# Two 16-head attention stages on one core: row maxima subtracted by another engine in layer 0, output sums joined differently in layer 1

## The reference

```python
# layer 0
scores = jnp.einsum('bhsd,bhtd->bhst', q, k) * scale
attn = jax.nn.softmax(scores, axis=-1)
out = jnp.einsum('bhst,bhtd->bhsd', attn, v)      # then times WO
# layer 1: rotary q and k, and a bias by distance
dist = jnp.abs(pos[None, :] - pos[:, None])
kb = -p * jnp.log1p(a * dist)
attn = jax.nn.softmax(scores + kb[None], axis=-1)
out = jnp.einsum('bhqk,bhkd->bhqd', attn, v)      # then times out_w.T
```

## Time and profile before

| what | value |
|---|---|
| median of three runs | 3134.81 us |
| the profiled execution's own time | 3134.13 us |
| its span, first to last instruction | 3132.3 us |
| mean granted TensorE clock | 0.962 |
| busy: PE / DVE / ACT / POOL | 2869.8 / 2307.5 / 1428.2 / 2439.6 us |
| attention in layer 0, first to last exponential | 239.3 to 1449.3 us |
| attention in layer 1, first to last exponential | 1815.0 to 3107.4 us |

### The profile page before, as it was taken

One profiled execution on the slowest core, in us unless ns is written; L12 is line 12 of the kernel. 1 busy time (PEld: TensorE's weight loads), 2 busy tenths in 40 slices (PEclk: granted clock), 3 DMA queues, 4 the chain that ended last, 5 costly groups with the idle time before them and its releaser, 6 DMA issues. The chain is left out here.

```text
span 3132.3 us, 46995 instructions
## 1 busy us (share of the span) xinstructions
PE 2869.8 (92%) x18168; PEld 1166.3 (37%) x18168; DVE 2307.5 (74%) x3507; ACT 1428.2 (46%) x1633; POOL 2439.6 (78%) x1141
## 2 busy tenths in 40 slices
PE   5949999999999999996499489999999999999997
PEld 3413434444444444343364123333333333333333
DVE  6545555555555555553339699999999999999996
ACT  4324555455554555453122244555555555555553
POOL 0008999999999999996238468888888888888887
PEclk9969999999999999998699699999999999999998
DMA  4250111111111111100213501111111111111100
GB/s 107 95 177 5 34 33 34 33 28 28 28 28 28 28 28 28 28 1 6 87 30 134 186 1 54 54 54 54 54 54 54 54 54 54 54 54 54 54 1 14
DMA packets 63823, 155.31 MB, mean 50 GB/s; under 512 B 18017, under 2 KB 33770, under 8 KB 61426
## 3 DMA queue, kind: packets, MB, share of 16 engines
q1 hardware_dynamic: 62578, 150.20, 17.4%
q0 software_dynamic: 1024, 2.10, 0.2%
HBM read 113.34 MB, written 38.93 MB: 49 GB/s over the span
## 5 line engine op out<-in xcount | busy, mean ns | idle before, releaser
L864 POOL TENSOR_TENSOR a_total<-a_total,room 128x1024 f32<-128x1024 f32 x768 | 1813.3, 2361 | 142.9 <-ACT room L757 37.4
L791 DVE TENSOR_REDUCE a_mx<-a_jb 128x1 f32<-128x1024 f32 x512 | 626.9, 1224 | 508.6 <-PE a_jb L630 508.6
L667 PE MATMUL a_ov<-room,va 128*64 128x512 f32 x4096 | 991.6, 605 | 0.0
L750 ACT ACTIVATE room<-room,sscale 128x1024 f32<-128x1024 f32 x512 | 588.3, 1149 | 650.9 <-DVE room L811 650.7
L757 ACT ACTIVATE room<-a_st,sscale 128x1024 f32<-128x1024 f32 x512 | 548.8, 1110 | 556.7 <-PE a_st L656 556.7
L786 DVE CUSTOM_DVE_ANT_0 a_junk<-a_jb,a_tab 128x1024 bf16<-128x1024 f32 x512 | 623.6, 1218 | 51.3 <-PE a_jb L630 35.1
L811 DVE TENSOR_TENSOR room<-a_st,a_tab 128x1024 f32<-128x1024 f32 x512 | 623.8, 1219 | 5.2 <-PE a_st L656 3.0
L629 PE MATMUL a_jb<-a_kh,a_qh 64*128 64x512 f16 x1024 | 396.8, 388 | 102.2 <-DMA a_tab<-bias_line 31.2
L864 POOL TENSOR_TENSOR a_total<-room 128x1024 f32<-128x1024 f32 x128 | 302.3, 2362 | 182.7 <-ACT room L750 136.1
L656 PE MATMUL a_st<-a_qh,a_kh 64*128 64x512 f16 x2048 | 394.9, 382 | 21.0 <-DVE room L811 21.0
L667 PEld LDWEIGHTS a_ov<-room,va 128*64 128x64 f32 x4096 | 248.4, 136 | 423.7 <-issue 363.8
(11 more groups left out here) (208 smaller groups left out, 2119.1 us busy)
## 6 DMA issues: line engine op xcount, KB each, us to landing
a_tab<-bias_line SPq DMA_DIRECT2D x16, 1984.0 KB, 12.6
...
```

The costliest lines, as they stand in the source:

```text
L667: last = nc.tensor.matmul(ov[t * DH:(t + 1) * DH, :], k.va[:, 2 * s + t, h * DH:(h + 1) * DH], prob[:, step % RING, t * QC:(t + 1) * QC], ...
L750: nc.scalar.activation(prob[:, r, :], prob[:, r, :], ACT.Exp, scale=k.sscale[:, layer:layer + 1])\
L791: nc.vector.reduce_max(mx[:, j // 2, j % 2:j % 2 + 1], jb[:, :], AX.X).then_inc(max_done, 1)
L864: nc.gpsimd.tensor_tensor(t, first, prob[:, step % RING, :], ALU.add).then_inc(summed, 1)
```

## The change

In layer 0, at six of the eight steps of a chunk (all but 0 and 4, `by_row`), the fourth round of the scores is gone. VectorE subtracts the maximum instead, from `rows`, and writes to the ring (`subtract_maxima`); ScalarE's exponential then works in place. For this `rows` must hold the maximum in all partitions, so ScalarE's division writes 512 columns. In both layers GpSimd keeps two running sums, adds to them in turn, joins them and folds into `total`: seven full adds and one half, as before. Row sums and projection are now one block each in a chunk (`SUM_STEP`, `OUT_STEP`): sums at step 3, projection at step 7 in layer 0 and step 5 in layer 1, where the transpose moves from step 5 to step 1. In layer 1 ScalarE scales the product into `part` and GpSimd adds it to `acc`. In the prologue the maxima go round three buffers (`jb` and both `st`), and they wait only for the high parts of q and k, whose low parts have a semaphore of their own and are issued after them.

The diff, cut to its core:

```diff
...
-ROW_STEP, OUT_STEPS = 5, (3, 7)
+SUM_STEP, ROW_STEP, OUT_STEP = (3, 3), (5, 1), (7, 5)
...
-rs = m.sb(g + "rs", [P, 2, 2])
-total = m.sb(g + "total", [P, 2, 2 * QC])
+rs = m.sb(g + "rs", [P, 4])
+sums, total = m.sb(g + "sums", [P, 2, 2 * QC]), m.sb(g + "total", [P, QC])
...
+sum_step, row_step, out_step = SUM_STEP[layer], ROW_STEP[layer], OUT_STEP[layer]
+lowered = None if bias else m.sem(g + "lowered")
...
-loads = 8 + (1 if bias else 0)
...
+def scratch(n, j):
+    i = NJ * n + j
+    return jb[:, :] if i >= FIRST or i % 3 == 2 else st[:, i % 3, :]
+
 def summed_by(step):
     n, s = divmod(step, NS)
-    return pool_adds * n + min(max(1, s), pool_adds)
+    return pool_adds * n + (1, 1, 2, 2, 3, 4, 5, 6)[s]
+
+def by_row(step):
+    return bias or step % 4 == 0
+
+def lowerings(steps):
+    return steps - (steps + 3) // 4
...
-            sp.dma_start(ql[low, at], k.qk_low[0, pr][half, :]).then_inc(loaded, 16)
-            sp.dma_start(kl[low, at], k.qk_low[1, pr][half, :]).then_inc(loaded, 16)
...
+        if h == 0:
+            sp.wait_ge(loaded, 16 * loads)
+        for low in (slice(0, DH), slice(DH, P)):
+            sp.dma_start(ql[low, at], k.qk_low[0, pr][half, :]).then_inc(low_loaded, 16)
+            sp.dma_start(kl[low, at], k.qk_low[1, pr][half, :]).then_inc(low_loaded, 16)
...
         if j == 0 and n % NC == 0:
             pe.wait_ge(loaded, 16 * loads * (n // NC + 1))
-        if NJ * n + j >= 1:
+        if NJ * n + j >= FIRST:
             pe.wait_ge(max_done, NJ * n + j)
+        elif NJ * n + j >= 3:
+            pe.wait_ge(max_done, NJ * n + j - 2)
+        o = scratch(n, j)
...
-        if n >= 2:
-            pe.wait_ge(proj_done, 2 * (n - 2) + 1)
+        if bias and n >= 3:
+            pe.wait_ge(proj_done, n - 2)
+        if not bias and n >= 2:
+            pe.wait_ge(rs_done, n - 1)
...
-        if step >= 2:
+        if n % NC == 0 and s == 0:
+            pe.wait_ge(low_loaded, 16 * 4 * (n // NC + 1))
+        if step >= 2 and by_row(step - 2):
             pe.wait_ge(st_read, step - 1)
-        for r, (keys, queries) in enumerate(((kh, qh), (kh, ql), (kl, qh), (lower, rows))):
+        elif step >= 2:
+            pe.wait_ge(lowered, lowerings(step - 1))
+        else:
+            pe.wait_ge(max_done, FIRST)
+        rounds = ((kh, qh), (kh, ql), (kl, qh), (lower, rows))[:4 if by_row(step) else 3]
...
+    def sums_of(n):
+        pe.wait_ge(folded, n + 1)
+        pe.wait_ge(row_done, min(n + (3 if bias else 2), NCH))
+        if n >= 1:
+            pe.wait_ge(proj_done, n)
+        for q in range(4):
+            last = nc.tensor.matmul(xb[:, q:q + 1], total[:, q * P:(q + 1) * P], k.ones[:, 0:1],
+                                    start=(q == 0), stop=True, skip_group_check=True)
+        last.then_inc(sum_ready, 1)
+
+    def project(n):
+        pe.wait_ge(ov_saved, n + 1)
+        pe.wait_ge(rs_done, n + 1)
+        pe.wait_ge(row_done, min(n + 3, NCH))
+        for q in range(4):
+            last = nc.tensor.matmul(xb[:, q * P:(q + 1) * P], osb[:, q * P:(q + 1) * P], k.wo[:, n // NC, :],
+                                    start=True, stop=True)
         last.then_inc(proj_ready, 1)
...
-        if s == ROW_STEP and n + 1 < NCH:
+        if s == row_step and n + 1 < NCH:
             row(n + 1)
-        if s in OUT_STEPS and n >= 1:
-            project(n - 1, OUT_STEPS.index(s))
+        if s == sum_step and n >= 1:
+            sums_of(n - 1)
+        if s == out_step and n >= 1:
+            project(n - 1)
...
-        nc.scalar.activation(m4w[:, :, 0:DH + 1:DH], m4[:, :].unsqueeze(2).broadcast_to([P, 4, 2]), ACT.Copy,
+        wide = m4w[:, :, 0:DH + 1:DH] if bias else m4w[:, :, :]
+        nc.scalar.activation(wide, m4[:, :].unsqueeze(2).broadcast_to([P, 4, 2 if bias else P]), ACT.Copy,
                              scale=1.0 / MAXROW).then_inc(m4_done, 1)
...
+        elif not by_row(step):
+            act.wait_ge(lowered, lowerings(step + 1))
+            nc.scalar.activation(prob[:, r, :], prob[:, r, :], ACT.Exp, scale=k.sscale[:, 0:1])\
                .then_inc(exp_done, 1)
...
+    def scale(n):
+        act.wait_ge(proj_ready, n + 1)
+        if n >= 1:
+            act.wait_ge(accumulated, n)
+        for q in range(4):
+            last = nc.scalar.activation(part[:, q * P:(q + 1) * P], xb[:, q * P:(q + 1) * P], ACT.Copy,
+                                        scale=rs[:, q:q + 1])
+        last.then_inc(proj_done, 1)
...
-            if s == 2 and n + 1 < NCH:
+            if s == (0 if bias else 2) and n + 1 < NCH:
                 divide_maxima(n + 1)
-            if s == ROW_STEP and n + 1 < NCH:
+            if s == row_step and n + 1 < NCH:
                 row(n + 1)
+            if bias and s == out_step and n >= 1:
+                scale(n - 1)
...
+    def subtract_maxima(n, s):
+        step = NS * n + s
+        ve.wait_ge(st_ready, step + 1)
+        if s == 1:
+            ve.wait_ge(row_done, n + 1)
+        if step >= RING:
+            ve.wait_ge(pv_done, step - RING + 1)
+            ve.wait_ge(summed, summed_by(step - RING))
+        p = prob[:, step % RING, :].rearrange("p (t q) -> p t q", t=2)
+        x = st[:, step % 2, :].rearrange("p (t q) -> p t q", t=2)
+        high = rows[:, n % 2, :].unsqueeze(1).broadcast_to([P, 2, QC])
+        nc.vector.scalar_tensor_tensor(p, high, -float(MAXROW), x, ALU.mult, ALU.add).then_inc(lowered, 1)
...
+    def invert(n):
+        ve.wait_ge(sum_ready, n + 1)
+        if n >= 1:
+            ve.wait_ge(proj_done, n)
+        nc.vector.reciprocal(rs[:, :], xb[:, 0:4]).then_inc(rs_done, 1)
+
+    def accumulate(n):
+        ve.wait_ge(proj_ready, n + 1)
+        for q in range(4):
+            a = k.acc[:, (n % NC) * 4 + q, :]
+            last = nc.vector.scalar_tensor_tensor(a, xb[:, q * P:(q + 1) * P], rs[:, q:q + 1], a,
                                                   ALU.mult, ALU.add)
         last.then_inc(proj_done, 1)
...
+            if s % 2 == 1 and not by_row(s):
+                subtract_maxima(n, s)
             if n + AHEAD < NCH:
                 maxima(n + AHEAD, s)
-            if s in OUT_STEPS and n >= 1:
-                invert(n - 1, OUT_STEPS.index(s))
-                accumulate(n - 1, OUT_STEPS.index(s))
-    for e in range(2):
-        invert(NCH - 1, e)
-        accumulate(NCH - 1, e)
+            if s % 2 == 0 and not by_row(s):
+                subtract_maxima(n, s)
+            if s == sum_step and n >= 1:
+                invert(n - 1)
+            if not bias and s == out_step and n >= 1:
+                accumulate(n - 1)
+    invert(NCH - 1)
+    if not bias:
+        accumulate(NCH - 1)
...
+    def add_part(n):
+        pool.wait_ge(proj_done, n + 1)
+        if n >= NC:
+            pool.wait_ge(accumulated, n - NC + 1)
+        a = flat(k.acc[:, (n % NC) * 4:(n % NC + 1) * 4, :])
+        nc.gpsimd.tensor_tensor(a, a, part[:, :], ALU.add).then_inc(accumulated, 1)
+
     for n in range(NCH):
-        t = total[:, n % 2, :]
-        if n >= 2:
-            pool.wait_ge(proj_ready, 2 * (n - 1))
-        for s in range(1, pool_adds + 1):
+        for i, s in enumerate((1, 3, 4, 5, 6, 7)):
             step = NS * n + s
+            a = sums[:, (n + i) % 2, :]
             pool.wait_ge(exp_done, step + 1)
-            first = prob[:, (step - 1) % RING, :] if s == 1 else t
-            if s >= 2:
-                pool.wait_ge(summed, pool_adds * n + s - 1)
-            nc.gpsimd.tensor_tensor(t, first, prob[:, step % RING, :], ALU.add).then_inc(summed, 1)
+            if i >= 2:
+                pool.wait_ge(summed, pool_adds * n + i - 1)
+            if i == 1 and n >= 1:
+                pool.wait_ge(folded, n)
+            first = a if i >= 2 else prob[:, (step - 1) % RING, :]
+            nc.gpsimd.tensor_tensor(a, first, prob[:, step % RING, :], ALU.add).then_inc(summed, 1)
+        pool.wait_ge(summed, pool_adds * n + 6)
+        a = sums[:, n % 2, :]
+        nc.gpsimd.tensor_tensor(a, a, sums[:, (n + 1) % 2, :], ALU.add).then_inc(summed, 1)
         pool.wait_ge(summed, pool_adds * (n + 1))
-        nc.gpsimd.tensor_tensor(t[:, 0:QC], t[:, 0:QC], t[:, QC:2 * QC], ALU.add).then_inc(folded, 1)
+        if n >= 1:
+            pool.wait_ge(sum_ready, n)
+        nc.gpsimd.tensor_tensor(total[:, :], a[:, 0:QC], a[:, QC:2 * QC], ALU.add).then_inc(folded, 1)
+        if bias and n >= 1:
+            add_part(n - 1)
+    if bias:
+        add_part(NCH - 1)
...
```

More of the change, by code:

```diff
@@ L656, in scores @@
                         last = nc.tensor.matmul(st[:, step % 2, t * QC:(t + 1) * QC], w, x,
-                                                start=(r == 0), stop=(r == 3))
+                                                start=(r == 0), stop=(r == len(rounds) - 1))
                 last.then_inc(st_ready, 1)
@@ L728, in _ @@
                 values(NCH - 1, s)
-            for e in range(2):
-                project(NCH - 1, e)
+            sums_of(NCH - 1)
+            project(NCH - 1)
```

65 lines of the change are left out of this document (27 added, 38 removed).

## The result

The changed kernel takes 3154.69 us (median of four runs, 3150.8 to 3157.51), the one before 3134.62 in the runs beside it: ratio 1.0063, 95% interval 1.0045 to 1.008. It is slower, by 20 us; 3148, 13 us slower, was forecast, with a range of 3104 to 3161.

The account below looks back on a forecast made before the run. Bound: TensorE's list in layer 0, the one-buffer maxima loop in layer 1; after the change, hand-overs. On 3134.1 us: layer 0 +51.5 - 2.7, prologues and tails -15.3 and -12.2, layer 1 -8: +13.3, so 3148 (3104 to 3161).

Parts of the forecast that it names:

- The forecast's case: Main case, chance 0.55: layer 0 slows through hand-overs and the fold wait, total 3148 us, own range 3138 to 3160.
- Pairs in layer 0: Layer 0, time per pair of steps from 2 and 3 on: 5.68 with the fold wait, 4.37, 5.13, 4.65 us.
- Steady: Layer 0's repeating chunks: 19.83 us each, +0.83 us over 62 chunks, +51.5 us.
- The wait for the fold: Layer 0, steps 2 and 3: TensorE's row sums wait 0.84 us for GpSimd's fold, ready at 12.64, wanted at 11.80.
- fold in time: Rival, chance 0.30: fold ready 0.84 us earlier than chained, layer 0 at 19.28 us a chunk, total 3114 us.
- The subtraction: Layer 0, six new VectorE instructions a chunk: 1.22 us each, 1.14 apart, like L811, not slowed by GpSimd.
- the rival of 3.36 us: Rival, chance 0.06: GpSimd slows every second layer 0 subtraction to 3.36 us, +398 us, total about 3546.
- no hand-over binds: Rival, chance 0.09: engines overlap freely, layer 0 at 17.7 and layer 1 at 19.1 us a chunk, total 2950.
- Layer 1: Layer 1's steady chunks, paced by the one-buffer maxima loop: 20.22 us, -0.13 over 62 chunks, -8 us.
- the warning that nothing would be saved: Perfetto Trace Analysis: VectorE and GpSimd share a port, so layer 1's moved accumulation saves nothing, losing 8 us of gain.
- Prologues: Start of each layer: three-buffer maxima -11.2 us, fewer awaited loads -4.5; sums -15.3 and, with layer 1's tail, -12.2.
- the ends of layer 0: Layer 0's first chunk has no row sums, -0.8 us; the last two have no maxima and are GpSimd's, -1.9.

Follow-up runs that it names:

- the filled kernel: The changed kernel plus three matmuls, their result overwritten, in each chunk of layer 0 where TensorE waits for the fold: 3147.49 us.
- the kernel with alternate half clock: The changed kernel, but in layer 0 VectorE takes the maxima tile ahead of the subtraction at odd steps too: 3194.08 us.
- the one run with single values in layer 1: The changed kernel, but in layer 1 TensorE takes values one step at a time instead of two steps after every second step: 3137.61 us.
- The filled kernels: The changed kernel, and it with the maxima tile first at odd steps, each with three unused matmuls before layer 0's fold wait: 3147.49 and 3138.5 us.

## Why the prediction was right

The forecast's case happened, and each step can be compared.

- Pairs in layer 0: 5.68, 4.37, 5.13, 4.65 us predicted; from the maxima's starts (900.51, 906.19, 910.55 and on) 5.68, 4.36, 5.11, 4.62. Steady +0.83 a chunk predicted, +0.73 measured, because the prediction subtracted 19.00 and the average of before is 19.04, and the last pairs are 0.01 to 0.03 shorter.
- The wait for the fold: 0.84 us predicted, 0.72 found; without it 19.28 predicted, 19.19 in the kernel without the join. The rival "fold in time" needed 0.84 us and is excluded by 55 waits of one size.
- The subtraction: 1.22 us taken, 1.214 measured, 384 times. This excludes the rival of 3.36 us, which was a single instruction: the other 31 of L453 take 1.21 to 1.22. The rule of the Trainium skill (SBUF — State Buffer, "Who interferes with whom") that an instruction with one SBUF input isn't blocked holds in these rows.
- The rival "no hand-over binds" (2950) is excluded by rows in which both engines wait in every chunk.
- Layer 1: 20.22 predicted, 20.20 found. The total is better than its parts: the pairs were forecast at 4.77, 5.19, 5.49 and 4.77 us and are 4.87, 5.22, 5.33 and 4.78 in a chunk of 20.19. Moving the accumulation to GpSimd did no harm: VectorE's L881 takes 1.217 us beside it, as L811 did (1.219), so the warning that nothing would be saved did not come true. No run took the parts of layer 1's change apart.
- Prologues: the first exponential of layer 0 comes at 223.53 instead of 239.26, -15.7 (-15.3 predicted); layer 1's prologue, from TensorE's last instruction ahead of it to the first exponential, gives -14.5 (-14.2 without the tail).
- Mis-sized: the ends of layer 0. The first chunk was put at -0.8; the first interval behind the prologue went from 17.95 to 19.75 us, +1.8, as it runs in the fold's loop too. The last two chunks were put at -1.9, as GpSimd's list alone; the last interval went from 17.74 to 22.60, +4.9. TensorE waits 2.6 us for the fold there and runs partly at half clock, while GpSimd itself waits 3.6 us for exponentials: a loop sets the pace there too, and no list.
- Missing: the clock, 5 x 1.65 = 8.3 us of the profiled run; by the filled kernel 7 us of the median. Without it the time is 3147.5.

That this lies on the forecast of 3148 is partly luck, because errors cancel. In the profiled run of the filled kernel layer 0 takes 1264.02 us from first to last exponential, 53.9 more than before. Of these the steady part is 62 x 0.73 = 45.3 us (51.5 predicted), the ends 8.6 (-2.7 predicted); all else gives -40.1 (-35.5 predicted). The sum is +13.8, where +13.3 was predicted. What is not luck are the pairs, the wait for the fold and the prologues, each within 0.5 us.

What stays open: what decides which idle time lowers the clock. TensorE's busy share from 300 to 1400 us is the same, 93%, in the kernel with alternate half clock, in the changed one (four stretches there), in that with the sums at step 5 (none) and in the one run with single values in layer 1 (none there, with the same code in layer 0). With the sums at step 5 TensorE even waits longer at one place, 0.81 us ahead of a maxima tile, without half clock. The filled kernels show that in steady chunks the idle time ahead of the row sums is needed for it, not what else is.
